# Attention and ternary-FFN layer on eight cores: x fetched as f32 by SP's queue and cast by ACT, in place of casting transfers on POOL's queue

## The reference, cut to what matters

```python
def attn(x, w_qkv, w_out):            # x: 8 x 4096 x 1024, 16 heads of 64
    q, k, v = split(x @ w_qkv)
    scores = q @ k.T / 8, causal
    return (softmax(scores) @ v) @ w_out
def ternary_linear(x, w):             # w -> sign(w) where |w| > 0.5 mean|w|, else 0
    return (x / rms(x)) @ w_t.T
x = layernorm(x + attn(x, w_qkv, w_out))
x = layernorm(x + ternary_linear(gelu(ternary_linear(x, w_up)), w_down))
```

## Time and profile before

| | |
|---|---|
| median of 3 runs | 2260.82 us (2260.28 to 2261.11) |
| the profiled execution's own time | 2259.11 us |
| its span (first to last instruction, slowest core) | 2257.2 us |
| spans of the 8 cores | 2249.8 to 2257.2 us |
| granted TensorE clock, all cores | 0.990 to 0.992 |
| PE busy | 2135.0 us (95%) |
| ACT busy | 1349.5 us (60%) |
| DVE busy | 1237.7 us (55%) |
| POOL busy | 355.3 us (16%) |

### The profile page before, as it was taken

The page is one execution under the profiler, slowest core; times in us unless marked ns, Lnnn a source line. Parts: engine busy times, 40 slices in busy tenths (PEclk is TensorE's granted clock), DMA queues, the critical chain, the costliest instruction groups (busy, mean ns, idle before and its releaser), DMA issues.

```text
span 2257.2 us, 54506 instructions; the slowest of 8 cores (2249.8 to 2257.2 us)
## 1 busy us (share of the span) xinstructions
PE 2135.0 (95%) x21250; PEld 1313.1 (58%) x21250; DVE 1237.7 (55%) x2100; ACT 1349.5 (60%) x1436; POOL 355.3 (16%) x574
## 2 busy tenths in 40 slices
PE   5999999998899999889999999999999999999998
PEld 2555555555455555466566656656656656566665
DVE  2455555677777533365566555645635545445654
ACT  1589888888788898732444444455465565755111
POOL 3222121222222122101100110110110110101110
PEclk9999999999999999989999999999999999999999
DMA  9135343353545113311000101100101100101100
GB/s 155 34 118 155 114 131 128 111 169 122 155 146 162 42 23 106 125 53 45 32 29 36 50 20 36 41 27 32 39 20 30 47 20 20 47 5 39 38 20 19
DMA packets 77946, 154.70 MB, mean 69 GB/s; under 512 B 27392, under 2 KB 45952, under 8 KB 76672
## 3 DMA queue, kind: packets, MB, share of 16 engines
q1 hardware_dynamic: 70880, 134.44, 17.8%
q0 software_dynamic: 6816, 16.78, 4.7%
HBM read 134.42 MB, written 33.55 MB: 74 GB/s over the span
## 4 chain that ended last, share of the span: by engine, by line
PE 84%; DVE 6%; ACT 5%; issue 4%; DMA 1%; DVEq 0%; POOL 0%; SPq 0%; ACTq 0%; POOLq 0%
PE mm L76 60%; PE sc L76 13%; PE pv L76 11%; ACT pb L76 3%; ACT L76 1%; DVE kt L76 1%; DVE wneg L76 1%; DMA xT<-xt 1%; DVE nrm L76 1%; DVE ast L76 1%; DMA yb<-x 1%; DVE vs L76 0%; DVE qt L76 0%; DVE pb L76 0%; DVE yb L76 0%
## 5 line engine op out<-in xcount | busy, mean ns | idle before, releaser
L76 ACT ACTIVATE pb<-sc,bias 128x1024 bf16<-128x1024 f32 (+3 forms) x1152 | 1160.7, 1042 | 449.8 <-PE sc L76 434.6
L76 PE MATMUL mm<-wdn,hT 128*128 128x512 fp8e4 x2048 | 479.3, 380 | 0.0
L76 PEld LDWEIGHTS pv<-vs,pb 128*128 128x128 bf16 x8448 | 365.5, 98 | 174.6 <-issue 48.0
L76 PE MATMUL pv<-vs,pb 128*128 128x65 bf16 x8448 | 410.1, 194 | 29.0 <-DVE ast L76 16.7
L76 ACT ACTIVATE hT<-mm 128x512 bf16<-128x512 f32 x256 | 152.9, 597 | 343.3 <-PE mm L76 342.7
L76 PEld LDWEIGHTS mm<-wdn,hT 128*128 128x128 bf16 x2048 | 186.6, 98 | 243.7 <-issue 51.7
L76 PE MATMUL mm<-xT,wq 128*128 128x512 bf16 x1024 | 307.9, 391 | 15.5 <-DMA xT<-xt 15.5
L76 PE MATMUL sc<-qt,kt 64*128 64x512 bf16 (+3 forms) x1440 | 270.0, 372 | 3.0 <-ACT pb L76 2.6
L76 PE MATMUL mm<-xnT,wupa 128*128 128x256 bf16 x2048 | 231.5, 274 | 2.3 <-ACT hT L76 1.3
L76 PEld LDWEIGHTS mm<-xnT,wupa 128*128 128x128 fp8e4 x2048 | 198.2, 98 | 28.7 <-issue 4.3
L76 DVE TENSOR_TENSOR hsq<-hT 128x512 f32<-128x512 bf16 x240 | 166.0, 692 | 56.2 <-ACT hT L76 52.1
(11 more groups left out here) (63 smaller groups left out, 1765.6 us busy)
## 6 DMA issues: line engine op xcount, KB each, us to landing
wr<-w_up SPq DMA_DIRECT2D x64, 512.0 KB, 3.6
wr<-w_down SPq DMA_DIRECT2D x64, 512.0 KB, 3.6
yb<-x SPq DMA_DIRECT2D x32, 512.0 KB, 3.2
out<-yb SPq DMA_DIRECT2D x32, 512.0 KB, 2.6
xT<-xt POOLq DMA_DIRECT2D x16, 512.0 KB, 35.9
wq<-w_qkv POOLq DMA_DIRECT2D x24, 256.0 KB, 8.9
att_s<-ast SPq DMA_DIRECT2D x40, 128.0 KB, 2.8
atto<-att_s SPq DMA_DIRECT2D x8, 640.0 KB, 4.2
```

What stands on the lines that cost most here:

```text
L76: ins = ops[op](*args, **kw)
```

## The change

x no longer goes over POOL's queue. SP's queue fetches each chunk as two f32 transfers of 128x2048 into a stage: even chunks lie in the bytes of slots 2 and 3 of `kt`, odd ones in slots 2 and 3 of `vs`. From there ACT casts it to `xT` in four instructions of 128x1024 (`AF.Copy`); of chunk 0 DVE does the first and the third. A stage is fetched anew when the four casts of two chunks earlier are done. The casts of chunk c + 1 stand at the start of `qkv(0, c)`. The constants are loaded behind chunk 0, with idn and tri last. The memset of the ones in `vs` is cut in two, and the part for slots 2 and 3 is put ahead of pair 2's first tile. PE's order is unchanged, but its wait for x is now for blocks of two `ch`.

```diff
-    for dst, src in ((idn, idn_h), (tri, tri_h), (blk, blk_h), (o64, o64_h),
-                     (onef, onef_h), (pw, pw_h)):
-        ctok = Y.dma(rings["c"], dst[:], src[:])
...
-    def load_x(c, half):
-        x_tok[c, half] = G.dma(
-            rings["x"], xT[:, c, 4 * half:4 * half + 4],
-            xt_h[c, :, 2048 * half:2048 * half + 2048]
-            .rearrange("p (c n) -> p c n", n=512))
-
-    load_w(0, 1)
-    load_x(0, 0)
-    load_x(0, 1)
-    load_w(0, 0, 2)
+    def stage(c, first, n):
+        if c % 2 == 0:
+            return bass.AP(kt32, S + first, [[2 * S, 128], [1, n]])
+        return bass.AP(vs32, NT * 130 + first, [[2 * NT * 130, 128], [1, n]])
...
+    def load_x(c):
+        if c < NCH:
+            if c >= 2:
+                Y.after(*[x_tok[c - 2, i] for i in range(4)])
+            for half in range(2):
+                xr32_tok[c, half] = Y.dma(
+                    rings["x"], stage(c, 2048 * half, 2048),
+                    xt_h[c, :, 2048 * half:2048 * half + 2048])
+
+    def cast_x(c):
+        if c < NCH:
+            for i in range(4):
+                dst = xT[:, c, 2 * i:2 * i + 2, :].rearrange(
+                    "p c n -> p (c n)")
+                if c == 0 and i % 2 == 0:
+                    V.after(xr32_tok[c, i // 2])
+                    V.put("tensor_copy", dst, stage(c, 1024 * i, 1024))
+                    x_tok[c, i] = V.done()
+                else:
+                    A.after(xr32_tok[c, i // 2])
+                    A.put("activation", dst, stage(c, 1024 * i, 1024),
+                          AF.Copy)
+                    x_tok[c, i] = A.done()
+            load_x(c + 2)
+
+    load_w(0, 1, 0, 2)
     load_w(1, 1, 0, 2)
-    for c in range(1, NCH):
-        for half in range(2):
-            load_x(c, half)
...
+    load_x(0)
+    for dst, src in ((blk, blk_h), (o64, o64_h), (onef, onef_h), (pw, pw_h),
+                     (idn, idn_h), (tri, tri_h)):
+        ctok = Y.dma(rings["c"], dst[:], src[:])
+    load_x(1)
+    cast_x(0)
...
+        if n == 0:
+            cast_x(c + 1)
+        if n == 2 and c == 0:
+            V.after(x_tok[NCH - 2, 3], x_tok[NCH - 1, 3])
+            nonlocal ones_tok
+            ones_tok = ones(2)
...
-                T.after(x_tok[c, ch // 4])
+                T.after(x_tok[c, ch // 2])
```

More of the change, by code:

```diff
@@ L315, in load_w, with ones @@
                 wqkv_h[p, part].rearrange("p (c n) -> p c n", n=128))
-    def load_x(c, half):
-        x_tok[c, half] = G.dma(
-            rings["x"], xT[:, c, 4 * half:4 * half + 4],
-            xt_h[c, :, 2048 * half:2048 * half + 2048]
-            .rearrange("p (c n) -> p c n", n=512))
-    load_w(0, 1)
-    load_x(0, 0)
-    load_x(0, 1)
-    load_w(0, 0, 2)
-    load_w(1, 1, 0, 2)
-    for c in range(1, NCH):
-        for half in range(2):
-            load_x(c, half)
-    V.put("memset", bass.AP(vs, 64, [[4 * NT * 130, 128], [65, 4 * NT * 2]]),
-          1.0)
-    ones_tok = V.done()
+    kt32 = kt.bitcast(F32)
+    vs32 = vs.bitcast(F32)
+    def stage(c, first, n):
+        if c % 2 == 0:
+            return bass.AP(kt32, S + first, [[2 * S, 128], [1, n]])
+        return bass.AP(vs32, NT * 130 + first, [[2 * NT * 130, 128], [1, n]])
+    xr32_tok = {}
+    def load_x(c):
[22 more added lines that the diff above has]
+    load_w(0, 1, 0, 2)
+    load_w(1, 1, 0, 2)
+    load_x(0)
[4 more added lines that the diff above has]
+    cast_x(0)
+    def ones(first):
+        V.put("memset", bass.AP(vs, 64 + first * NT * 130,
+                                [[4 * NT * 130, 128], [65, 2 * NT * 2]]), 1.0)
+        return V.done()
+    ones_tok = ones(0)
     q_tok, k_tok, v_tok, b_tok, qs_tok = {}, {}, {}, {}, {}
```

## The result

The changed kernel takes 2271.04 us (median of 6 runs, 2268.83 to 2272.63), against 2260.97 us of the kernel before (6 runs): 10.1 us more. The ratio is 1.0039, with a 95% interval of 1.0025 to 1.0054. So it is slower, by 0.25 to 0.54%. The profiled execution has a span of 2269.2 us on its slowest core, core 5; the other cores lie between 2263.1 and 2267.8, and the median of all eight is 2266.2 (before: 2255.4).

What follows compares the result with a forecast made beforehand. The prediction took PE's fixed order to bound the kernel (84% of the chain). Stalls of 9.3 us less a start gain of 2.1 made 7.2 us slower, 2268.0 us at the median; range 2260 to 2273.

Steps and rivals of the forecast that it cites:

- The stalls of PE behind the casts: Pair 0, chunks 2 to 5: sc matmuls wait for an exponent delayed by four casts; 9.3 us in sum.
- What comes behind a stall: After each stall in pair 0: no second stall follows and none of the delay is given back; nothing added.
- The start: Up to the first exponent: it starts at 30.2 instead of 32.34, a gain of 2.1 us.
- The second exponent: Its chunk 2 casts end at 36.5, due at 36.8: costs nothing, with 0.3 us to spare.
- the other edits: DVE's casts and memsets, POOL's fewer issues, PE's split waits: cost nothing, over before the constants land.
- The start did not pay for the casts: Rival: chunk 1 lands at 24.8, first exponent at 27.0, 5.3 us early; total about 2263.5, not slower; chance 0.20.
- Tables were not loaded: Rival: each block of casts on ACT loads a table twice, 15.5 us on top, total 2283.5; chance 0.04.
- The rival of the constants: At the start PE waits for constants, then runs at low clock; first exponent 1.2 us later, total 2271.3; chance 0.12.
- the signs: In the changed profile: casts near 1.1 us, stalls of 2 to 4, first exponent near 30, constant delay from chunk 6.

Runs made afterwards that it cites:

- b1_start: Changed kernel with casts singly behind exponents, constants on POOL's queue between pair 0's and pair 1's weights, chunk 1's second-half casts after the first exponent; 2268.66 us.
- a1_blocks: Kernel before, its own transfers of x kept, plus five blocks of four unused ACT copies where the change casts chunks 3 to 7; 2271.26 us, ratio 1.0045.

## Why the prediction was right, point by point

The forecast was 2268.0 and slower; measured was 2271.04, inside the range, with a difference of 10.1 us where I had 7.2. The mechanism that I named, PE waiting for exponents behind blocks of casts, is there, in the chunks named. But it makes 7.1 of the 10.1 us, and that the total comes so near is in part luck: the stalls were 2.2 us smaller than forecast, the start 2.6 us worse, and some 5 us came from the low clock behind the stalls, for which my sum had nothing. These terms come to 13 us at the end of chunk 5 on core 5; by the end of the kernel some 2 us of the delay are gone, which no run explains.

**The stalls of PE behind the casts: right in kind and place, 7.1 us for 9.3.** None in chunk 1, as said; none in chunk 2, where I had 0.4; 1.38, 2.51 and 3.22 us in chunks 3 to 5, where I had 2.1, 3.2 and 3.6. The term that was mis-sized is the cast. I took 1.11 us from the exponent; four casts in a row take 3.88, 0.97 each. The Trainium skill ("ScalarE: Activation LUTs", What ACT_TABLE_LOAD costs) gave an estimate of 0.95, and by it stalls of 7.0 us. The trace agrees with it.

**What comes behind a stall: left out at this place.** I wrote that behind a stall no second one follows and that the delay is the stall. The trace shows 5.5 us in the median, 6.0 on the slowest core, beyond the waits, all but 0.35 of it at the low level of the clock. I had the mechanism, but only as a rival, and for the start. My evidence against it was one idle stretch of 3.35 us after which the matmuls ran at full clock. The same idle stretch stands on all 8 cores of that trace, and on four of them (0, 1, 3 and 4) the matmuls behind it were slow. The row of core 1:

```profile
31.94 2.66 PE L76 MATMUL mm<-wq,xT 128*128 128x128 bf16 x24
```

They take 1.50 us on core 2. So the trace that I had already held the answer, that the clock falls behind such a stretch on some cores and on others not.

**The start: a gain of 2.1 us forecast, none there.** On the cores that I read, the first exponent moved from 32.34 (core 2) to 31.02 (core 5). But core 2 had one of the latest starts of the 8 before (29.4 to 32.4, median 30.7), and after they lie between 30.9 and 32.9, median 31.5: 0.8 us later, not 2.1 earlier. The steps were near: the norm matmul at 23.3 behind tri (said: 22.5), casts ending at 31.1 (said: 30.2). The step that failed is the comparison with a single core. Against the median of before, a norm matmul at 22.5 is 0.4 us late and not 1.2 early. A slip of arithmetic did little: a third of the way from 29.0 to 24.8 is 27.6 and not 28.0, which would have made the gain 2.5.

**The second exponent and the other edits at nothing: right.** On core 5 ACT is idle 0.22 us ahead of the second exponent, for PE, when the casts of chunk 2 are done. No load of a table stands between casts and exponents: there are 28 in the trace, as before. The Trainium skill ("ScalarE: Activation LUTs", Table sets: the hidden batching unit) says that copy is in every set. The trace agrees. An exception to "nothing" may be the 0.35 us in chunk 5, which the variants built on the changed kernel have and those built on the kernel before have not.

**Against the rivals.** The start did not pay for the casts. Tables were not loaded. The rival of the constants was right about the start where the forecast was not: PE did wait for them, on all 8 cores, on six of them the matmuls behind ran in part at the low clock, and the first exponent came 0.8 us later than before, where this rival has 1.2. Its total, 2271.3, is nearer than mine as well, but that is chance: it took the stalls at 9.3 us and nothing behind them.

**Of the signs** by which I would know, one is not clean: the delay is 12.4 us at the end of pair 0's chunk 5 and 10.8 at the end of the kernel. It is still 11.5 near 950 us. The cores' ends scatter by 5 us, and where the rest goes I did not settle.

## What to carry to other kernels

An engine that looks 60% busy may have no room where a block of new work is put. Before placing it, compare its length with the slack at that place: the time from the end of the exponent before the block to the start of the matmuls that wait for the exponent behind it, less that exponent. The same work set singly where ACT was idle cost nothing that the times can tell. Where an idle stretch of PE is forecast, the matmuls behind it should be priced at both levels of the clock. And where cores differ by more than the effect, the first thing to read is the same row on all of them: both misses of this forecast, the start and the clock, came from reading one core.

## What the runs showed of the hardware that I had not expected

- Behind a wait of PE in an otherwise full stretch the granted clock fell on some cores and not on others, in one execution of one program: behind 1.05 us on 0 of 8 cores, behind 1.37 on 14 of 24, behind 1.57 on 5 of 88, behind 2.50 on 21 of 24, behind 3.21 on 16 of 16. A fall cost 1.3 to 1.6 us in most cases, and up to some 2.7 behind the longer waits.
- At the start the 24 small matmuls behind the wait for tri took 1.50 us on two cores of the changed kernel and 1.9 to 2.7 on six; in b1_start, behind waits of 4.5 to 7.0 us, they took 2.8 on all 8.
- ACT's copy of 128x1024 has a mean of 1.05 us and takes 0.97 in a row of four, the same from f32 (1048 ns) as from bf16 (1044 ns in a1_blocks).
- A transfer of 1 MB on SP's queue landed 6.8 us after its issue when it was the first of all (issued at 1.06), and 13.3 us after when it was issued at 3.8, behind the six constants and with POOL's weights under way.
